# Scan stage: turned states as three rounded products, split by ScalarE and GpSimd, with the input sum on GpSimd

## The chip, the cores and the metric

The kernel runs on one core of one Trainium2 chip. The metric is device time in microseconds (us) of the whole program. Engines are named TensorE (PE in the profile, with its weight loads as PEld), VectorE (DVE), ScalarE (ACT), GpSimd (POOL) and SyncE (SP, which issues the DMAs).

## The reference, cut to what matters

`x` has shape (16, 1024, 256), float32. The reference adds four branches in turn, each to `x` and each of a layer norm of `x`: a state space layer, a feed-forward coupling, causal attention, and the feed-forward coupling again. The change touches the first one alone:

```python
# h = layernorm(x); Lbar = mag * exp(i * Lam_imag * dt), one complex decay for each of 64 states
nr = Lbar_r * sr - Lbar_i * si + bur          # bur, bui = h @ (dt * B_real).T, h @ (dt * B_imag).T
ni = Lbar_r * si + Lbar_i * sr + bui
y = SR @ C_real.T - SI @ C_imag.T + D * h
out = y @ W_out.T + b_out                     # x = x + out
```

The kernel turns the rotating complex recurrence into a real one. It multiplies the inputs by cos and sin of the angle of each step, adds the two products, runs a scan with a real decay, and multiplies the scanned states by cos and sin again. The outputs are matrix products with weights into which `C` and `W_out` are folded.

## The kernel before

The stage is `ssm_phase`. It has 32 chunks, two for each of the 16 sequences, of 512 steps of 256 features. A chunk is held as four tiles of 128 steps. Buffers are doubled: chunk n uses set k = n mod 2. In the steady state each engine works through one slot n of the main block in a fixed, written-out order; there is no planner, and the engines meet through semaphores alone.

- TensorE (`slot`, L493): `turn(n+1)` (L160) transposes the normalised rows (8 records at L166). `project(n+1)` (L462) makes the two input products `ssm_bu`, 8 matmuls of 512 columns with the rounded transposed input (L469) and 4 with its remainder (L474). `out(n)` (L478) makes four output tiles at L488: each has 4 products of `xnT` and 2 of `xnT_lo` with the rounded skip weights, and 2 full float32 products, `w_cos` with `out_cos_w` and `w_sin` with `out_sin_w`. A float32 product is two records in the trace.
- VectorE (`slot`, L435): `low(n+1)` (L145) takes the remainder of the transposed input, `normalise(n+2)` (L123) makes statistics and moments, `scan(n+1)` (L405) makes `u_cos`, `u_sin`, their sum `u` (L411), the scan (L413), `w_cos` (L419) and `w_sin` (L420). Then `scale(n+2)` (L136) normalises the rows in four `tensor_scalar` instructions (L141), and `residual(n)` (L422) adds the output to `xb` (L427).
- ScalarE: `evacuate(n)` (L151) copies and rounds the transposed input (L158), two instructions for each chunk.
- GpSimd: `chunk(n)` (L385) makes `var_eps` and `rstd` in `rstds` (L115, L117 and L121), then `xb` = `x` + bias in `residual_bias` (L393), which waits for `y` of chunk n-2.
- SyncE loads and stores the chunks (L361, L365).

"Rounded" is the type float32r, a float32 that TensorE takes in one pass. The skip weights are already held as a rounded part and the rounded remainder (`skip_parts`). In the block ahead of the main one VectorE makes these parts at L312 and L315, and the output weights at L316 and L317.

Of the kernel before, what the change touches and what calls it, by code (L numbers as in the profile page):

```python
# [57 lines left out]
def ssm_phase(nc, sem, identf, x, x1, log_lam, lam_imag, b_real, b_imag, c_real, c_imag, d_skip, log_dt,  # L58
# [15 lines left out]
    with ExitStack() as ctx:  # L74
        def sb(name, shape, dt=F32):
            return ctx.enter_context(nc.sbuf_tensor("ssm_" + name, shape, dt))
# [26 lines left out]
        w = [sb(f"w{k}", [P, CH]) for k in range(2)]  # L103
        w_cos = [sb(f"w_cos{k}", [P, CH]) for k in range(2)]
        w_sin = [sb(f"w_sin{k}", [P, CH]) for k in range(2)]
        turned_ps = ctx.enter_context(nc.psum_tensor("ssm_turned", [P, KT, CH], F32))
# [3 lines left out]
        (stats_done, moments_done, eps_added, rstd_ready, xn_ready, turned, xnT_ready, xnT_lo_ready, bu_ready, u_parts, u_ready,  # L110
         w_ready, w_turned, out_ready, xb_ready, y_ready, const_ready) = [sem("ssm_" + n) for n in (
             "stats_done", "moments_done", "eps_added", "rstd_ready", "xn_ready", "turned", "xnT_ready", "xnT_lo_ready", "bu_ready",
             "u_parts", "u_ready", "w_ready", "w_turned", "out_ready", "xb_ready", "y_ready", "const_ready")]

        def rstds(pool, n, k, old):  # L115
            pool.wait_ge(moments_done, n + 1)
# [53 lines left out]
        with ExitStack() as pre:  # L170
# [40 lines left out]
            with nc.Block() as block:  # L211
# [31 lines left out]
                def _(dve):  # L243
# [71 lines left out]
                        v.tensor_tensor(parts[1][:, :, :], w[:, :, :], parts[0][:, :, :], ALU.subtract)  # L315
                    v.tensor_copy(out_cos_w[:, :], m_ps[:, 0, 0:D])  # L316
                    step(v.tensor_copy(out_sin_w[:, :], m_ps[:, 1, 0:D]))  # L317

                @block.scalar
                def _(act):  # L320
# [31 lines left out]
        with nc.Block() as block:  # L352
# [29 lines left out]

            @block.gpsimd
            def _(pool):
                def chunk(n, it, k, old):  # L385
                    rstds(pool, n, k, old)
                    residual_bias(n, it, k, old)

                def residual_bias(n, it, k, old):
                    pool.wait_ge(x_loaded[k], 16 * it + 16)  # L390
                    if old:
                        pool.wait_ge(y_ready, n - 1)
                    nc.gpsimd.tensor_tensor(xb[k][:, :, :], xt[k][:, :, :],  # L393
                                            bias_row[:, :].unsqueeze(1).to_broadcast([P, TT, D]),
                                            ALU.add).then_inc(xb_ready, 1)

                residual_bias(0, 0, 0, False)
                chunk(1, 0, 1, False)
                with pool.Fori(1, n_steps) as it:
                    for k in range(2):  # L400
                        chunk(2 * it + k, it, k, True)

            @block.vector
            def _(dve):
                def scan(n, k, old):  # L405
                    cos_k, sin_k = cos_t[:, k * CH:(k + 1) * CH], sin_t[:, k * CH:(k + 1) * CH]
                    dve.wait_ge(bu_ready, n + 1)
                    nc.vector.tensor_tensor(u_cos[:, :], bu_ps[k][:, 0, :], cos_k, ALU.mult)
                    nc.vector.tensor_tensor(u_sin[:, :], bu_ps[k][:, 1, :], sin_k, ALU.mult).then_inc(u_parts, 1)
                    dve.wait_ge(u_parts, n + 1)  # L410
                    nc.vector.tensor_tensor(u[:, :], u_cos[:, :], u_sin[:, :], ALU.add).then_inc(u_ready, 1)  # L411
# [7 lines left out]
                    nc.vector.tensor_tensor(w_cos[k][:, :], w[k][:, :], cos_k, ALU.mult)  # L419
                    nc.vector.tensor_tensor(w_sin[k][:, :], w[k][:, :], sin_k, ALU.mult).then_inc(w_turned, 1)  # L420
# [10 lines left out]
                scale(dve, 1, 1, False)  # L431
                scan(0, 0, False)


                def slot(n, it, k, old, more):  # L435
                    low(dve, n + 1, 1 - k)
                    if more:
                        normalise(dve, n + 2, it + 1, k, True)
                    scan(n + 1, 1 - k, old or k == 1)
                    if more:  # L440
                        scale(dve, n + 2, k, True)
                    residual(n, it, k, old)

                slot(0, 0, 0, False, True)
                slot(1, 0, 1, False, True)
                with dve.Fori(1, n_steps - 1) as it:
                    for k in range(2):
                        slot(2 * it + k, it, k, True, True)
                it = n_steps - 1
                slot(2 * it, it, 0, True, False)  # L450
                residual(2 * it + 1, it, 1, True)

            @block.scalar
            def _(act):
                evacuate(act, 1, 1, False)
                with act.Fori(1, n_steps) as it:
                    for k in range(2):
                        evacuate(act, 2 * it + k, k, True)

            @block.tensor  # L460
            def _(pe):
# [1758 lines left out]
```

## Time and profile before

| what | value |
|---|---|
| median of 3 runs | 3762.95 us (3755.66 to 3763.63) |
| the profiled execution's own time | 3763.16 us |
| its span | 3761.3 us |
| busy, share of the span | PE 95%, PEld 62%, DVE 79%, ACT 58%, POOL 44% |
| the first stage | up to about 380 us of the span |

A row of a timeline gives the start, the duration, the engine, the line, the operation, what it writes and reads, how many were merged, and in brackets the idle time of the engine before it with what released it. Busy times of TensorE overlap, since matmuls are pipelined, so distances between starts are the better measure there. A row of busy time by stretches gives the stretch, its length, then the busy time and the instructions of PE, PEld, DVE, ACT and POOL, the granted clock of TensorE as a share, the DMA share and GB/s.

### The profile page before, as it was taken

To read this page: it belongs to the slowest core of one execution; us is meant where nothing else is said; L and a number is where in the kernel's file an instruction comes from. 1 tells how busy PE (TensorE), PEld (TensorE's weight loads), DVE (VectorE), ACT (ScalarE), POOL (GpSimd) and SP (SyncE) were. 2 spreads that over 40 slices of the span, in tenths; PEclk is the share of its full clock that TensorE was granted. 3 is DMA by queue.
4 is the path that set the end of the run, shared out by engine and by line. 5 is a ranking of instruction groups with operands and counts; after the bars stand their busy time and mean duration, and the time that the engine had idled before them with its cause. 6 is when DMAs were issued, how large, how long until landed. Compare 5 with 4: busy or idle time off the path is not lost. (4 is left out here: it accounts for less than half of the span.)

```text
span 3761.3 us, 76026 instructions
## 1 busy us (share of the span) xinstructions
PE 3560.0 (95%) x25550; PEld 2347.9 (62%) x25550; DVE 2952.9 (79%) x9275; ACT 2183.7 (58%) x4151; POOL 1666.4 (44%) x2027
## 2 busy tenths in 40 slices
PE   6999899999689999999999999999999998999997
PEld 5888666666455665566656656655666555666664
DVE  8998666766688888888888888888888893676775
ACT  1110456655337766766676667667667665656654
POOL 2332123223345556656555565565565511223323
PEclk9999899999879999999999999999999999999999
DMA  2333112111497978787887879788887832121211
GB/s 74 100 98 109 57 46 68 54 59 35 116 140 111 126 115 129 120 127 123 122 127 119 132 116 126 116 119 123 124 134 121 120 41 80 40 68 46 68 46 45
DMA packets 694291, 361.16 MB, mean 96 GB/s; under 512 B 297905, under 2 KB 660913, under 8 KB 693937
## 3 DMA queue, kind: packets, MB, share of 16 engines
q1 hardware_dynamic: 693936, 356.62, 53.5%
q8 instruction: 200, 3.28, 0.4%
q14 instruction: 155, 1.26, 0.2%
HBM read 204.49 MB, written 150.99 MB: 95 GB/s over the span
## 5 line engine op out<-in xcount | busy, mean ns | idle before, releaser
L1862 ACT ACTIVATE att_probs<-att_s 128x512 f32<-128x512 f32 x2304 | 1212.5, 601 | 461.2 <-PE att_s L2001 234.4
L1737 DVE CUSTOM_DVE_ANT_0 att_s<-att_s,att_above 128x384 f32<-128x384 f32 (+3 forms) x2048 | 950.2, 519 | 132.8 <-PE att_s L1981 127.1
L1981 PE MATMUL att_s<-att_ks,att_qs 48*128 48x512 f32 (+3 forms) x3072 | 896.0, 401 | 5.7 <-DVE att_maxima L1740 3.6
L2001 PE MATMUL att_s<-att_qs,att_ks 49*128 49x512 f32 (+3 forms) x3072 | 852.4, 373 | 20.5 <-DVE att_maxima L1737 5.2
L2001 PEld LDWEIGHTS att_s<-att_qs,att_ks 49*128 49x128 f32 x3072 | 487.6, 186 | 464.0 <-ACT att_probs L1862 271.6
L1740 DVE TENSOR_REDUCE att_maxima<-att_s 128x1 f32<-128x512 f32 x1024 | 661.9, 684 | 98.3 <-PE att_s L1981 93.2
L2029 PE MATMUL att_o_ps<-att_probs,att_vs 128*32 128x512 f32 (+3 forms) x6144 | 620.5, 497 | 25.1 <-ACT att_probs L1862 22.1
L1981 PEld LDWEIGHTS att_s<-att_ks,att_qs 48*128 48x128 f32 x3072 | 485.9, 189 | 26.4 <-DVE att_maxima L1737 8.9
L1097 PE MATMUL ffn_h2p<-ffn_h,ffn_w 128*128 128x512 f32 x768 | 365.0, 598 | 3.0 <-ACT ffn_h L968 0.9
L1951 PE MATMUL att_s<-att_mask,att_places 64*128 64x128 bf16 (+1 forms) x2560 | 327.7, 212 | 0.0
L1737 DVE DVE_READ_ACCUMULATOR2_ANT att_maxima<- 128x1 f32 x2048 | 293.0, 143 | 0.0
L946 ACT ACTIVATE ffn_uv<-ffn_uvp 128x512 f32<-128x512 f32 x256 | 153.1, 598 | 237.5 <-PE ffn_uvp L1072 237.5
L2029 PEld LDWEIGHTS att_o_ps<-att_probs,att_vs 128*32 128x32 f32 x6144 | 145.9, 108 | 222.9 <-issue 159.6
L1564 POOL CAST att_qs<-att_staged 113x1024 fp32r<-113x1024 f32 x128 | 253.7, 2005 | 0.0
L976 ACT ACTIVATE ffn_h<-ffn_turned,ffn_b 128x512 f32<-128x512 f32 x384 | 241.9, 684 | 13.5 <-PE ffn_turned L1088 11.6
L1564 POOL CAST att_ks<-att_staged 113x1024 fp32r<-113x1024 f32 x126 | 249.7, 2000 | 0.0
L968 ACT ACTIVATE ffn_h<-ffn_h2p,ffn_b 128x512 f32<-128x512 f32 x192 | 132.0, 687 | 197.8 <-PE ffn_h2p L1097 197.8
L1088 PEld LDWEIGHTS ffn_turned<-identf,ffn_uv 128*128 128x128 f32 x1536 | 174.8, 142 | 75.5 <-issue 53.9
L158 ACT ACTIVATE ssm_xnT<-ssm_turned 128x512 fp32r<-128x512 f32 x64 | 34.9, 595 | 313.7 <-PE ssm_turned L166 313.7
L1088 PE MATMUL ffn_turned<-identf,ffn_uv 128*128 128x128 f32 x1536 | 201.8, 274 | 10.2 <-DVE ffn_uv L823 8.0
L823 DVE SCALAR_TENSOR_TENSOR ffn_uv<-ffn_uv,ffn_c_pos 128x256 f32<-128x256 f32 x512 | 209.3, 483 | 2.3
L691 POOL TENSOR_TENSOR ffn_var_eps<-ffn_moments,ffn_eps 128x4 f32<-128x4 f32 x64 | 13.3, 208 | 433.4 <-DVE ffn_moments L776 433.4
(292 smaller groups left out, 6384.8 us busy)
## 6 DMA issues: line engine op xcount, KB each, us to landing
att_staged<-qk_scratch SPq DMA_DIRECT2D x768, 128.0 KB, 7.6
qk_scratch<-att_parts SPq DMA_DIRECT2D x128, 512.0 KB, 3.4
ffn_x<-x SPq DMA_DIRECT2D x64, 512.0 KB, 5.2
ssm_x<-in_L_attn_a_x_dram SPq DMA_DIRECT2D x32, 512.0 KB, 3.7
x<-ssm_y SPq DMA_DIRECT2D x32, 512.0 KB, 3.0
x<-ffn_y SPq DMA_DIRECT2D x32, 512.0 KB, 2.9
att_x<-x SPq DMA_DIRECT2D x32, 512.0 KB, 7.4
v_scratch<-att_v_tok SPq DMA_DIRECT2D x32, 512.0 KB, 5.3
```

What stands on the lines that cost most here:

```text
L823: last = v.scalar_tensor_tensor(out=new[:, t, 0:D], in0=old[:, t, D:2 * D], scalar=c_pos[i][j][:, t, k:k + 1], in1=old[:, t, 0:D], op0=ALU ...
L976: last = a(h1[k][:, f, :], turned_ps[:, f, :], ACT.Gelu, bias=b1[:, f:f + 1])
L1088: last = pe.transpose(turned_ps[:, f, t * P:(t + 1) * P], of[:, t, f * P:(f + 1) * P], identf[:, :])
L1097: last = mm(h2_ps[:, :], w2[:, f, :], h1[k][:, f, :], start=(f == 0), stop=(f == KT - 1))
L1564: last = g.tensor_copy(stack[0:ROWS, :].rearrange("p (t c) -> p t c", c=HD)[:, e * n:(e + 1) * n, :], staged[side][0:ROWS, :, e * n:(e + 1 ...
L1737: last = v.tensor_tensor_reduce(scores, scores, above[:, CH - w:CH], 1.0, -3.0e38, ALU.add, ALU.max, to)
L1740: last = v.tensor_reduce(to, scores, AX.X, ALU.max)
L1862: a(probs[u % PROBS][2 * g + p][:, 0:n], bank[:, 0:n], ACT.Exp).then_inc(exp_done, 1)
L1951: last = mm(blocks[:, at, GROUP * half:GROUP * (half + 1)], places[rows, 2 * (1 - k) + half, :], mask[rows, 1 - k, 0:len(cols), :], start= ...
L1981: last = mm(bank[:, col:col + w], rows_of(qs[buf], g, KROWS, p, BT * blk, BT * (blk + 1)), rows_of(ks[buf], g, KROWS, p, t0, t1), start=k ...
L2001: last = mm(bank[:, col:col + w], rows_of(ks[buf], g, SHIFT + 1, p, BT * j, BT * (j + 1)), rows_of(qs[buf], g, SHIFT + 1, p, t0, t1), star ...
L2029: last = mm(o_ps[32 * i:32 * i + 32, HD * (t0 - first_t):HD * (t1 - first_t)], vs[s][:, NBLK * head + j, :], probs[of % PROBS][i][:, col:c ...
```

## The change

The two float32 products of each output tile become six rounded ones. The weights `out_cos_w` and `out_sin_w` are split into two rounded parts ahead of the main block (four more VectorE instructions on 128x256). For the states, ScalarE rounds `w_cos` and `w_sin` (`round_turned`, after `evacuate` of the chunk behind), and GpSimd subtracts to get the remainders (`split`). TensorE's `out` waits for the second remainder. The sum `u` goes from VectorE to GpSimd (`add_parts`), and VectorE's `scale(n+2)` moves ahead of the scan, between `u_sin` and the wait for `u`.

```diff
+                def add_parts(n):
+                    pool.wait_ge(u_parts, n + 1)
+                    nc.gpsimd.tensor_tensor(u[:, :], u_cos[:, :], u_sin[:, :], ALU.add).then_inc(u_ready, 1)
+
+                def split(n, k):
+                    for m, turned_w in enumerate((w_cos[k], w_sin[k])):
+                        pool.wait_ge(w_hi_ready, 2 * n + m + 1)
+                        nc.gpsimd.tensor_tensor(w_lo[k][:, m, :], turned_w[:, :], w_hi[k][:, m, :].bitcast(F32),
+                                                ALU.subtract).then_inc(w_lo_ready, 1)
+
                 def chunk(n, it, k, old):
                     rstds(pool, n, k, old)
+                    add_parts(n - 1)
+                    split(n - 1, 1 - k)
                     residual_bias(n, it, k, old)
...
@@ VectorE, slot
-                    scan(n + 1, 1 - k, old or k == 1)
+                    turn_back(n + 1, 1 - k)
                     if more:
                         scale(dve, n + 2, k, True)
+                    scan(n + 1, 1 - k, old or k == 1)
                     residual(n, it, k, old)
...
@@ ScalarE
+                def round_turned(n, k):
+                    for m, turned_w in enumerate((w_cos[k], w_sin[k])):
+                        act.wait_ge(w_back, 2 * n + m + 1)
+                        nc.scalar.activation(w_hi[k][:, m, :], turned_w[:, :], ACT.Copy).then_inc(w_hi_ready, 1)
...
                         evacuate(act, 2 * it + k, k, True)
+                        round_turned(2 * it + k - 1, 1 - k)
...
@@ TensorE, out
-                    pe.wait_ge(w_turned, n + 1)
+                    pe.wait_ge(w_lo_ready, 2 * n + 2)
...
-                        terms += [(w_cos[k][:, cols], out_cos_w[:, :]), (w_sin[k][:, cols], out_sin_w[:, :])]
+                        terms += [(w_hi[k][:, m, cols], out_parts[i][:, m, :]) for m in range(2) for i in range(2)]
+                        terms += [(w_lo[k][:, m, cols], out_parts[0][:, m, :]) for m in range(2)]
```

`turn_back(n, k)` holds the two multiplications `u_cos` and `u_sin` that stood at the head of `scan`. For chunk 0 they stand after `scale(1)`. After the loop GpSimd does `add_parts` and `split` of the last chunk, and ScalarE its `round_turned`.

## Rows read from the trace of the kernel before

**Rows 1.** Busy time by stretches, in the steady stage.
```profile
60.00:160.00 100.00, 97.43 (x576) 84.98 (x575) 94.12 (x208) 9.78 (x18) 32.73 (x28) 1.00 0.31 99
```

**Rows 2.** Waits of VectorE and TensorE, 60 to 350 us: total, times, longest.
```profile
DVE ssm_y L427 <- PE ssm_out L488: 11.6, 28, 0.4
PE ssm_bu L469 <- ACT ssm_xnT L158: 7.8, 27, 0.3
```

**Rows 3.** Timeline of one slot, TensorE and ScalarE.
```profile
201.66 1.09 PE L166 MATMUL ssm_turned<-identf,ssm_xn 128*128 128x128 f32 x8
202.43 1.09 ACT L158 ACTIVATE ssm_xnT<-ssm_turned 128x512 fp32r<-128x512 f32 x2 [9.52 <-PE ssm_turned L166]
203.08 0.73 PE L469 MATMUL ssm_bu<-ssm_xnT,ssm_bu_p 128*128 128x512 f32 x2 [0.33 <-ACT ssm_xnT L158]
...
205.96 0.64 PE L488 MATMUL ssm_out<-ssm_skip_p,ssm_xnT 128*128 128x256 f32 x4
...
206.67 0.59 PE L488 MATMUL ssm_out<-ssm_out_cos_w,ssm_w_cos 128*128 128x256 f32 x2
...
207.34 0.82 PE L488 MATMUL ssm_out<-ssm_skip_p,ssm_xnT 128*128 128x256 f32 x4
...
212.25 1.04 PE L166 MATMUL ssm_turned<-identf,ssm_xn 128*128 128x128 f32 x8
```

**Rows 4.** Timeline of the same slot, VectorE.
```profile
201.96 1.23 DVE L427 TENSOR_TENSOR ssm_y<-ssm_out,ssm_xb 128x1024 f32<-128x1024 f32 x1 [0.43 <-PE ssm_out L488]
203.10 1.28 DVE L148 TENSOR_TENSOR ssm_xnT_lo<-ssm_turned,ssm_xnT 128x512 fp32r<-128x512 f32 x2
...
206.16 0.69 DVE L408 TENSOR_TENSOR ssm_u_cos<-ssm_bu,ssm_cos 128x512 f32<-128x512 f32 x1
...
207.48 0.69 DVE L411 TENSOR_TENSOR ssm_u<-ssm_u_cos,ssm_u_sin 128x512 f32<-128x512 f32 x1
208.21 1.22 DVE L413 TENSOR_TENSOR_SCAN ssm_w<-ssm_decay,ssm_u 128x512 f32<-128x512 f32 x1
209.46 0.69 DVE L419 TENSOR_TENSOR ssm_w_cos<-ssm_w,ssm_cos 128x512 f32<-128x512 f32 x1
...
210.67 1.38 DVE L141 TENSOR_SCALAR ssm_xn<-ssm_x,ssm_moments,ssm_rstd 128x256 f32<-128x256 f32 x4
212.45 1.22 DVE L427 TENSOR_TENSOR ssm_y<-ssm_out,ssm_xb 128x1024 f32<-128x1024 f32 x1 [0.40 <-PE ssm_out L488]
```

**Rows 5.** Timeline of the same slot, GpSimd.
```profile
203.33 2.42 POOL L393 TENSOR_TENSOR ssm_xb<-ssm_x,ssm_bias_row 128x1024 f32<-128x1024 f32 x1 [6.34 <-DVE ssm_y L427]
206.19 0.20 POOL L117 TENSOR_TENSOR ssm_var_eps<-ssm_moments,ssm_eps 128x4 f32<-128x4 f32 x1 [0.45 <-DVE ssm_moments L133]
206.47 1.01 POOL L121 TENSOR_TENSOR ssm_rstd<-ssm_var_eps,ssm_minus_half 128x4 f32<-128x4 f32 x1
```

**Rows 6.** Groups by line and form, GpSimd, whole span: busy, mean ns, idle before.
```profile
L1552 POOL TENSOR_TENSOR att_parts<-att_full,att_parts 128x512 fp32r<-128x512 f32 x116 | 148.6, 1281 | 9.3
```

**Rows 7.** Timeline at the head of the main block, GpSimd and VectorE.
```profile
37.39 2.35 POOL L393 TENSOR_TENSOR ssm_xb<-ssm_x,ssm_bias_row 128x1024 f32<-128x1024 f32 x1
37.46 3.41 DVE L141 TENSOR_SCALAR ssm_xn<-ssm_x,ssm_moments,ssm_rstd 128x256 f32<-128x256 f32 x4 [1.82 <-POOL ssm_rstd L121]
```

**Rows 8.** Timeline in the feed-forward stage, VectorE and GpSimd.
```profile
926.11 2.34 DVE L844 SCALAR_TENSOR_TENSOR ffn_y<-ffn_z,ffn_b_pos,ffn_y 128x128 f32<-128x128 f32 x1 [4.03 <-POOL ffn_y L729]
926.15 2.15 POOL L729 TENSOR_SCALAR ffn_y<-ffn_z,ffn_a_std,ffn_moments 128x256 f32<-128x256 f32 x4
```

**Rows 9.** Timeline of VectorE in the block ahead of the main one.
```profile
30.39 0.28 DVE L312 CAST ssm_bu_p<-ssm_bu_w 128x256 fp32r<-128x256 f32 x1
...
31.25 0.42 DVE L315 TENSOR_TENSOR ssm_bu_p<-ssm_bu_w,ssm_bu_p 128x256 fp32r<-128x256 f32 x1
```

**Rows 10.** Tile ssm_y: count, ns min/median/max, first and last start.
```profile
L427 DVE TENSOR_TENSOR ssm_y<-ssm_out,ssm_xb x32: 1224/1225/1226, 54.2 to 378.1; 128x1024 f32<-128x1024 f32 x32
```

**Rows 11.** Timeline of VectorE late in the stage.
```profile
359.79 1.23 DVE L427 TENSOR_TENSOR ssm_y<-ssm_out,ssm_xb 128x1024 f32<-128x1024 f32 x1 [0.40 <-PE ssm_out L488]
```

More of the change, by code:

```diff
@@ L105, in ssm_phase @@
         w_sin = [sb(f"w_sin{k}", [P, CH]) for k in range(2)]
+        w_hi, w_lo = [[sb(f"{n}{k}", [P, 2, CH], F32R) for k in range(2)] for n in ("w_hi", "w_lo")]
+        out_parts = [sb(f"out_p{i}", [P, 2, D], F32R) for i in range(2)]
         turned_ps = ctx.enter_context(nc.psum_tensor("ssm_turned", [P, KT, CH], F32))
@@ L110, in ssm_phase @@
         (stats_done, moments_done, eps_added, rstd_ready, xn_ready, turned, xnT_ready, xnT_lo_ready, bu_ready, u_parts, u_ready,
-         w_ready, w_turned, out_ready, xb_ready, y_ready, const_ready) = [sem("ssm_" + n) for n in (
+         w_ready, w_back, w_hi_ready, w_lo_ready, out_ready, xb_ready, y_ready, const_ready) = [sem("ssm_" + n) for n in (
              "stats_done", "moments_done", "eps_added", "rstd_ready", "xn_ready", "turned", "xnT_ready", "xnT_lo_ready", "bu_ready",
-             "u_parts", "u_ready", "w_ready", "w_turned", "out_ready", "xb_ready", "y_ready", "const_ready")]
+             "u_parts", "u_ready", "w_ready", "w_back", "w_hi_ready", "w_lo_ready", "out_ready", "xb_ready", "y_ready", "const_ready")]
         def rstds(pool, n, k, old):
@@ L317, in _ @@
                     step(v.tensor_copy(out_sin_w[:, :], m_ps[:, 1, 0:D]))
+                    turns = (out_cos_w, out_sin_w)
+                    for m, turn_w in enumerate(turns):
+                        last = v.tensor_copy(out_parts[0][:, m, :], turn_w[:, :])
+                    step(last)
+                    for m, turn_w in enumerate(turns):
+                        last = v.tensor_tensor(out_parts[1][:, m, :], turn_w[:, :], out_parts[0][:, m, :], ALU.subtract)
+                    step(last)
                 @block.scalar
@@ L401, in _, with turn_back @@
                         chunk(2 * it + k, it, k, True)
+                add_parts(n_chunks - 1)
+                split(n_chunks - 1, 1)
             @block.vector
             def _(dve):
+                def turn_back(n, k):
+                    cos_k, sin_k = cos_t[:, k * CH:(k + 1) * CH], sin_t[:, k * CH:(k + 1) * CH]
+                    dve.wait_ge(bu_ready, n + 1)
+                    dve.wait_ge(u_ready, n)
+                    nc.vector.tensor_tensor(u_cos[:, :], bu_ps[k][:, 0, :], cos_k, ALU.mult)
+                    nc.vector.tensor_tensor(u_sin[:, :], bu_ps[k][:, 1, :], sin_k, ALU.mult).then_inc(u_parts, 1)
                 def scan(n, k, old):
                     cos_k, sin_k = cos_t[:, k * CH:(k + 1) * CH], sin_t[:, k * CH:(k + 1) * CH]
[L407 to L411, printed above, removed]
                     dve.wait_ge(u_ready, n + 1)
@@ L418, in scan @@
                         dve.wait_ge(out_ready, n - 1)
-                    nc.vector.tensor_tensor(w_cos[k][:, :], w[k][:, :], cos_k, ALU.mult)
-                    nc.vector.tensor_tensor(w_sin[k][:, :], w[k][:, :], sin_k, ALU.mult).then_inc(w_turned, 1)
+                    nc.vector.tensor_tensor(w_cos[k][:, :], w[k][:, :], cos_k, ALU.mult).then_inc(w_back, 1)
+                    nc.vector.tensor_tensor(w_sin[k][:, :], w[k][:, :], sin_k, ALU.mult).then_inc(w_back, 1)
                 def residual(n, it, k, old):
@@ L431, in _ @@
                 scale(dve, 1, 1, False)
+                dve.wait_ge(bu_ready, 1)
+                cos_0, sin_0 = cos_t[:, 0:CH], sin_t[:, 0:CH]
+                nc.vector.tensor_tensor(u_cos[:, :], bu_ps[0][:, 0, :], cos_0, ALU.mult)
+                nc.vector.tensor_tensor(u_sin[:, :], bu_ps[0][:, 1, :], sin_0, ALU.mult).then_inc(u_parts, 1)
                 scan(0, 0, False)
@@ L454, in _ @@
             def _(act):
+                def round_turned(n, k):
+                    for m, turned_w in enumerate((w_cos[k], w_sin[k])):
+                        act.wait_ge(w_back, 2 * n + m + 1)
+                        nc.scalar.activation(w_hi[k][:, m, :], turned_w[:, :], ACT.Copy).then_inc(w_hi_ready, 1)
                 evacuate(act, 1, 1, False)
+                round_turned(0, 0)
                 with act.Fori(1, n_steps) as it:
@@ L458, in _ @@
                         evacuate(act, 2 * it + k, k, True)
+                        round_turned(2 * it + k - 1, 1 - k)
+                round_turned(n_chunks - 1, 1)
             @block.tensor
```

## The prediction

> **What bounds the stage now.** I read the busy time by stretches first, then the waits, then the timeline of one slot of each engine. Up to 380 us only this stage runs, and nothing else in the program changes, so only its length counts. Between 60 and 160 us TensorE is busy 97.4% at a granted clock of 1.00 (2.4 GHz) and VectorE 94.1%, while ScalarE has 10% and GpSimd 33% [rows 1]. Only two waits recur: VectorE's residual waits about 0.4 us for TensorE's output, 28 times, and TensorE about 0.3 us for ScalarE's copy, 27 times [rows 2]. So TensorE sets the pace and VectorE is close behind. The residual starts at 54.2 for chunk 0 [rows 10] and at 359.79 for chunk 29 [rows 11], 29 slots of 10.54 us.
>
> The slot shows how tight it is. TensorE goes from one transposition to the next in 212.25 - 201.66 = 10.59 us [rows 3]. VectorE's `scale` ends at 210.67 + 1.38 = 212.05, 0.2 us before the transposition that needs it [rows 3, 4]. GpSimd is idle most of the slot, with 2.42 + 0.20 + 1.01 us of work [rows 5].
>
> **What TensorE gains.** In the first output tile the six rounded products take 206.67 - 205.96 = 0.71 us, 0.118 each. The record at 207.34, the head of the second tile, is put some 0.2 early against the matmuls before it, so I take the whole: from 205.96 to 212.25 the four tiles take 6.29 us, 1.57 each [rows 3]. Twelve rounded products take 12 x 0.118 = 1.42, four tiles 5.67. That is 0.62 us less for each slot, if nothing else came in.
>
> **What VectorE gains.** The sum `u` and the wait for it go: 208.21 - 207.48 = 0.73 us [rows 4], and some 0.1 us of the wait before it. Without its wait of 0.43 a slot is about 10.1 us of work, so about 9.2 is left.
>
> **What GpSimd takes on.** Three instructions on 128x512 with two inputs in SBUF: one sum and two differences. The same form with the same types takes 1281 ns in the attention stage, 116 times [rows 6]. I take 1.28 us, and 1.25 from start to start, since on this engine the next one starts some 0.03 us before the end. GpSimd's work grows from 3.6 to 7.4 us a slot, well within 10.5. But its order now makes a loop, and I price that loop.
>
> **The blockade inside the loop.** `add_parts` follows `rstd` on GpSimd and reads two tiles in SBUF, and VectorE's `scale` is released by the same `rstd`. The head of the main block has this very meeting: GpSimd's `xb` starts at 37.39, the four `scale` instructions start at 37.46 and take 3.41 us [rows 7] instead of 1.38 [rows 4]. They lose 2.03 us to an instruction of 2.35, that is its duration less 0.32. In the feed-forward stage a VectorE instruction with two SBUF inputs takes 2.34 us while four GpSimd instructions run for 2.15 [rows 8]. So `scale` doesn't run beside the sum, it waits for it: 1.28 - 0.32 = 0.96 us. From below the price is nothing (the two overlap), from above it is the whole 1.28; I take 0.96, because rows 7 have the same two kinds of instruction in the same order.
>
> The Trainium skill, SBUF — State Buffer, section "Who interferes with whom", has the rule: VectorE in a two-port mode and GpSimd share one pair of ports, the one that issues first holds it for its whole instruction, and the other fully blocks. By that rule the sum with the blockade is 3784.5 us, and by the opposite (both run side by side) it would be 3772.5. Rows 7 agree with the rule. It speaks against putting the sum under `scale`.
>
> **The loop.** Let 0 be the start of the sum on GpSimd.
> - `scale` starts at 0.07 [rows 7], takes 1.30 up to the next start (1.38 less an overlap of 0.08 as between instructions elsewhere) and 0.96 more. The scan starts at 2.33.
> - `w_cos` starts 1.25 later and ends after 0.69 [rows 4]: 4.27. In every second chunk the scan is 0.06 longer; on the mean 4.30.
> - ScalarE starts 0.08 later (a handoff, estimated from 206.19 against the end of the moments) and hands on after 0.65, as 202.43 to 203.08 [rows 3]; GpSimd starts about 0.05 later still than TensorE did: 5.08.
> - The two differences, 1.25 each: 7.58. Then `xb`, which follows in GpSimd's order, 2.35 from start to start (2.40 less the overlap) [rows 5, 7]: 9.93.
> - `var_eps` to `rstd` 0.28, `rstd` 1.01 less 0.03 [rows 5]: 11.19. Then the next sum starts, since VectorE's `u_parts` are long there.
>
> In some slots `rstd` starts 0.08 later after `var_eps`, so I take 11.22 us a slot, 0.68 more than 10.54. `var_eps` doesn't wait for the moments in it: VectorE is at the residual at 2.33 + 1.25 + 0.61 + 0.60 = 4.79, at `low` 1.14 later, and has the moments 3.06 after that [rows 4], at 8.99, when `xb` holds GpSimd until 9.93. VectorE then stands still before `scale` for about 1 us a slot. TensorE starts its transposition at about 2.5, has projected by 7.7 (its last remainder products wait for `low`), and ends the output at 7.7 + 5.67 = 13.4, that is 2.2 in the next slot; it isn't on the path. The 0.62 us it saved go into idle time. Its idle pieces stay about 1 us, and I expect no drop of the clock; the bound above is a half clock for part of each slot, several us a slot, which no row of the steady stage supports.
>
> **The new wait of `out`.** It needs the second difference, at 5.08 + 2.53 = 7.61 plus a handoff. That ties with the end of the projection, so it costs nothing while the loop above rules. Queued behind it on TensorE are the next transpositions.
>
> **Head and tail.** Four more VectorE instructions on 128x256 ahead of the main block: starts 0.20 apart for casts and 0.34 for differences, with two semaphore steps, 1.3 us, with nothing to hide them [rows 9], where a start-to-start distance is 0.08 less than the duration. In the main block `scale(1)` no longer meets `xb` (it comes back 2.0 us), but the sum of chunk 0 comes after `scale(1)`, and the second `rstd` after both differences and `xb(1)`. From 37.42 + 1.3 I add 0.04 + 1.30 + 1.28 + 0.08 + 1.28 + 0.05 + 1.25 + 0.69 + 0.08 + 0.70 + 2.50 + 2.35 + 0.28 + 1.01 and come to 51.6, and the first residual at 51.6 + 4.8 = 56.4, against 54.2 [rows 10]: +2.2 us. At the end the last two chunks take 378.1 - 359.8 = 18.3 us now [rows 10, 11]; there the last sum follows `xb(31)` at 9.9, the second difference ends at about 16.5, the output takes 5.7, and the last residual starts 17.7 after that of chunk 29: -0.6 us.
>
> **The sum.** 29 x 0.68 = 19.7, + 2.2 - 0.6 = +21.3 us. On the profiled execution's 3763.16 us that gives 3784.5. That execution stands 0.2 us from the median of the runs shown, so the same number is compared with them.
>
> **Rivals.**
> - No blockade: `scale` runs beside the sum. The loop through GpSimd is then 11.22 - 0.96 + 0.1 = 10.4, and another one decides: `round_turned` stands behind `evacuate` on ScalarE. From a transposition's start to the end of the second copy is 203.52 - 201.66 = 1.86, the rounding with handoffs 0.70, the differences 2.53, the handoff 0.06, the output 5.67: 10.82 us [rows 3, 6]. That is 29 x 0.28 + 1.2 = +9.3, 3772.5 us. Against it stand rows 7.
> - VectorE wins the port: the sum then waits for all of `scale`, and the scan starts at 0.07 + 1.38 + 1.28 = 2.7 instead of 2.33. The slot is 11.6, the time 3796. For it: the two are released by the same instruction and 0.07 us decides. Against it: rows 7 show GpSimd first. The same page says that issue order decides who blocks, and that gives this case no other number.
> - The gain arrives: TensorE stays the pacer and its 0.62 us a slot come through, 29 x -0.62 + 1.6 = -16.4, 3747 us. This needs both differences before the projection ends, 4.3 us after the transposition's start, so each at 0.8 us or less instead of 1.28, and the loop through `xb` below 10. For it: GpSimd is idle two thirds of the slot now. Against it: 116 instructions of that form at 1281 ns.
> - The products don't become cheaper than they were: without a rounded rate for them TensorE would need 12 x 0.118 plus more, but the loop on GpSimd hides up to 0.3 us a slot of it; about 3785 to 3790.
>
> **Chances.** The forecast has 0.60, no blockade 0.14, VectorE first 0.12, the gain 0.08, the rest (TensorE dearer, clock) 0.06. The forecast's own spread is 3777 to 3791 (a slot of 11.0 to 11.45). The range reaches down to the case without blockade and up to that with VectorE first: 3769 to 3797. What can be told from no change here is about 0.2%, 7.5 us. Faster by more gets 0.08, within it 0.09 (the low side of the case without blockade), slower 0.83.
>
> **What would show it.** The distance between residuals in the steady stage: 11.2 us, against 10.8, 11.6 or 9.9 in the other cases. `scale` at L141's place would take about 2.3 us for four, starting 0.07 us after the sum; VectorE would wait about 1 us a slot for `rstd`; GpSimd's only long idle time, about 3.8 us, would stand before the first difference, ended by ScalarE; the output would take 5.7 us and TensorE be busy below 92%. A residual that still waits for the output, or `scale` at 1.38 beside the sum, would prove me wrong.

## The result and the profile after

The changed kernel takes 3789.17 us (median of 4 runs, 3782.70 to 3790.77), the kernel before 3760.01 us (median of 4, 3755.66 to 3763.63). The ratio is 1.0069, 95% interval 1.0056 to 1.0083. That is slower, clear of the noise but by less than 1%: about 26 us by the ratio, 29.2 between the medians. The forecast was 3784.5. The profiled execution took 3790.77 us with a span of 3788.9, 27.6 more than the span before.

The line of the residual's tile gives the length of the stage:

```profile
L452 DVE TENSOR_TENSOR ssm_y<-ssm_out,ssm_xb x32: 1214/1217/1225, 56.9 to 401.1; 128x1024 f32<-128x1024 f32 x32
```

Against 54.2 to 378.1 [rows 10] the first residual comes 2.7 us later, and the stretch from the first to the last grows from 323.9 to 344.2 us, by 20.3. Together 23.0 of the 27.6 us lie in the stage. The other 4.6 lie behind it, where both kernels execute the same instructions; they are taken up below, under "The rest of the span".

Busy time of the same stretch as [rows 1], then the waits of 60 to 360 us (total, times, longest):

```profile
60.00:160.00 100.00, 90.98 (x610) 77.64 (x610) 88.89 (x187) 20.67 (x36) 65.23 (x54) 1.00 0.30 92
```
```profile
POOL ssm_w_lo L401 <- ACT ssm_w_hi L488: 101.3, 27, 3.8
...
DVE ssm_xn L143 <- POOL ssm_rstd L123: 30.7, 27, 1.3
PE ssm_bu L512 <- DVE ssm_xnT_lo L150: 16.8, 26, 0.7
...
PE ssm_bu L507 <- ACT ssm_xnT L160: 7.8, 27, 0.3
```

TensorE fell from 97.4% to 91.0% and VectorE from 94.1% to 88.9%: neither is the bound any more. GpSimd is at 65%, so by busy time it isn't either. The waits show what is: VectorE stands still before the row scaling in every slot until GpSimd's `rstd` is there, and GpSimd stands still before its first difference until ScalarE has rounded. Each waits for the other in turn, which is a loop. VectorE's residual no longer waits for TensorE, as it did 28 times in [rows 2].

The timeline of one slot, VectorE, answers to [rows 4]:

```profile
202.68 1.22 DVE L452 TENSOR_TENSOR ssm_y<-ssm_out,ssm_xb 128x1024 f32<-128x1024 f32 x1
...
209.17 2.34 DVE L143 TENSOR_SCALAR ssm_xn<-ssm_x,ssm_moments,ssm_rstd 128x256 f32<-128x256 f32 x4 [1.18 <-POOL ssm_rstd L123]
211.43 1.27 DVE L438 TENSOR_TENSOR_SCAN ssm_w<-ssm_decay,ssm_w,ssm_u 128x512 f32<-128x512 f32 x1
212.74 0.69 DVE L444 TENSOR_TENSOR ssm_w_cos<-ssm_w,ssm_cos 128x512 f32<-128x512 f32 x1
...
213.95 1.21 DVE L452 TENSOR_TENSOR ssm_y<-ssm_out,ssm_xb 128x1024 f32<-128x1024 f32 x1
```

and GpSimd's, to [rows 5]:

```profile
209.10 1.28 POOL L396 TENSOR_TENSOR ssm_u<-ssm_u_cos,ssm_u_sin 128x512 f32<-128x512 f32 x1
214.17 1.29 POOL L401 TENSOR_TENSOR ssm_w_lo<-ssm_w_cos,ssm_w_hi 128x512 fp32r<-128x512 f32 x1 [3.78 <-ACT ssm_w_hi L488]
...
216.65 2.40 POOL L414 TENSOR_TENSOR ssm_xb<-ssm_x,ssm_bias_row 128x1024 f32<-128x1024 f32 x1
219.01 0.20 POOL L119 TENSOR_TENSOR ssm_var_eps<-ssm_moments,ssm_eps 128x4 f32<-128x4 f32 x1
219.29 1.01 POOL L123 TENSOR_TENSOR ssm_rstd<-ssm_var_eps,ssm_minus_half 128x4 f32<-128x4 f32 x1
220.27 1.29 POOL L396 TENSOR_TENSOR ssm_u<-ssm_u_cos,ssm_u_sin 128x512 f32<-128x512 f32 x1
```

Follow the loop once around. The sum starts at 209.10 and `scale` at 209.17, but `scale` takes 2.34 instead of 1.38, so the scan waits for it until 211.43. `w_cos` ends at 213.43, ScalarE rounds it, the two differences start at 214.17 and 215.41, `xb` follows, and the next `rstd` lets the next sum start at 220.27, 11.17 after the first. No instruction in this circle has slack, and between `scale` and the rounding there is a second way of the same length. TensorE's transposition waits for `scale` too (it starts 0.13 us after `scale` ends), and ScalarE's copies of it, which stand ahead of the rounding, end when `w_cos` is there (213.50 and 213.43). By these rows a faster scan alone would gain nothing; that wasn't tested.


```profile
212.41 1.09 ACT L160 ACTIVATE ssm_xnT<-ssm_turned 128x512 fp32r<-128x512 f32 x2 [8.97 <-PE ssm_turned L168]
213.46 0.63 ACT L488 ACTIVATE ssm_w_hi<-ssm_w_cos 128x512 fp32r<-128x512 f32 x1
```

TensorE, against [rows 3]: its output now takes from 205.72 to about 211.4.

```profile
205.72 0.64 PE L527 MATMUL ssm_out<-ssm_skip_p,ssm_xnT 128*128 128x256 f32 x4
...
207.15 0.63 PE L527 MATMUL ssm_out<-ssm_skip_p,ssm_xnT 128*128 128x256 f32 x4
...
211.64 1.09 PE L168 MATMUL ssm_turned<-identf,ssm_xn 128*128 128x128 f32 x8
```

### The profile page after: what moved, and what is told of

It is laid out like the page before. It is cut to its first block and busy times, and to the rows that moved or that the text cites. A ratio compares the mean times of both kernels' runs of the same rounds, so it can differ in the third digit from the quotient of the medians.

```text
span 3788.9 us, 76791 instructions
## 1 busy us (share of the span) xinstructions
PE 3564.4 (94%) x25806; PEld 2341.1 (62%) x25806; DVE 2952.6 (78%) x9247; ACT 2221.8 (59%) x4215; POOL 1784.0 (47%) x2123
## 3 DMA queue, kind: packets, MB, share of 16 engines
q14 instruction: 156, 1.28, 0.1%
## 5 line engine op out<-in xcount | busy, mean ns | idle before, releaser
L1127 PE MATMUL ffn_turned<-identf,ffn_uv 128*128 128x128 f32 x1536 | 202.5, 275 | 10.2 <-DVE ffn_uv L862 7.9
```

What stands on the lines that cost most here:

```text
L1127: last = pe.transpose(turned_ps[:, f, t * P:(t + 1) * P], of[:, t, f * P:(f + 1) * P], identf[:, :])
```

## The experiments

"First to last" below is from the start of the first residual to that of the last, 31 slots. "Steady slot" is the mean distance between the residuals of chunks 4 and 29, 25 slots; single slots differ from it, by up to 0.15 us in most kernels and by 0.55 in e9. (The prediction's 10.54 for the kernel before and 11.22 for the change count from chunk 0; counted so, the change measures 11.21.) Ratios are to the kernel before, run on the same chip, with the 95% interval. The experiments ran on four chips, on which the median of the kernel before is between 3755.8 and 3763.7 us, so rows are compared by ratio or by slot. The three single runs (e2, e6, e7) have no interval; the kernel before took 3755.8 there.

| kernel | us | ratio | first to last | steady slot |
|---|---|---|---|---|
| before | 3760.01 | 1 | 323.9 | 10.52 |
| after | 3789.17 | 1.0069 (1.0056 to 1.0083) | 344.2 | 11.20 |
| e1_sum_vector | 3771.54 | 1.0022 (1.0008 to 1.0037) | 331.5 | 10.76 |
| e2_half_sum | 3773.36 | one run | 332.7 | 10.76 |
| e3_products_alone | 3765.14 | 1.0004 (0.9990 to 1.0018) | 323.7 | 10.51 |
| e4_scale_first | 3764.95 | 0.9999 (0.9985 to 1.0012) | 322.0 | 10.48 |
| e5_both_alone | 3740.79 | 0.9939 (0.9920 to 0.9958) | 302.4 | 9.85 |
| e6_bias_late | 3814.97 | one run | 381.5 | 12.41 |
| e7_vector_first | 3793.13 | one run | 344.3 | 11.21 |
| e8_round_first | 3745.74 | 0.9974 (0.9957 to 0.9991) | 314.3 | 10.23 |
| e9_rows_on_scalar | 3768.84 | 1.0023 (1.0009 to 1.0037) | 327.1 | 10.70 |
| e10_mean_first | 3742.32 | 0.9944 (0.9926 to 0.9963) | 304.4 | 9.84 |
| e11_rows_halved | 3746.55 | 0.9954 (0.9940 to 0.9968) | 306.3 | 9.91 |

### e1: the sum back on VectorE

```diff
 GpSimd, chunk
-                    add_parts(n - 1)
...
 VectorE, turn_back
+                    dve.wait_ge(u_parts, n + 1)
+                    nc.vector.tensor_tensor(u[:, :], u_cos[:, :], u_sin[:, :], ALU.add).then_inc(u_ready, 1)
```

> The changed kernel with the sum u back on VectorE, between u_sin and scale; everything else as changed. Theory (the loop through GpSimd with the sum and the blockade in it sets the slot): scale falls back from 2.34 to 1.38 us for four, GpSimd's loop loses 1.25 for the sum and 0.96 for the blockade and is near 9.7, and the next loop decides, the one in which ScalarE rounds only behind its evacuation: 10.7 to 10.85 us from residual to residual, some 3770 to 3775 us. Rival (the blockade is a side effect, and the differences in front of the output's wait set the slot by themselves): the slot stays at 11.1 to 11.2 and the time near 3785.

Measured: `scale` back at 1.38, a slot of 10.76, 12.7 us less from first to last than the changed kernel. The sum on GpSimd costs 0.44 us a slot although its own blockade is 0.96, because a second loop stands right behind. VectorE's and ScalarE's timelines show it:

```profile
203.31 1.38 DVE L143 TENSOR_SCALAR ssm_xn<-ssm_x,ssm_moments,ssm_rstd 128x256 f32<-128x256 f32 x4 [0.91 <-POOL ssm_rstd L123]
```
```profile
205.90 1.09 ACT L160 ACTIVATE ssm_xnT<-ssm_turned 128x512 fp32r<-128x512 f32 x2 [8.65 <-PE ssm_turned L168]
206.87 0.63 ACT L486 ACTIVATE ssm_w_hi<-ssm_w_cos 128x512 fp32r<-128x512 f32 x1
```

The rounding stands behind the two copies, these behind the transposition, that behind the output of the chunk before, and that output behind the differences of the rounding. This is the loop of 10.82 us that the prediction priced under "no blockade". The expectation for e1 put GpSimd's own loop near 9.7, with the sum's 1.25 taken off as well as the blockade. That was wrong: `scale` waits for `rstd` and not for the sum, so the sum's own length isn't in the loop, only the blockade is (see e8).

### e2: the sum over half the columns

The other half of `u` stays zero, so half of the sum is left out.

```diff
-   nc.gpsimd.tensor_tensor(u[:, :], u_cos[:, :], u_sin[:, :], ALU.add)
+   nc.gpsimd.tensor_tensor(u[:, 0:CH // 2], u_cos[:, 0:CH // 2], u_sin[:, 0:CH // 2], ALU.add)
```

> The changed kernel with GpSimd's sum over half of the columns; the other half of u stays zero, so half of the sum is left out. Dose test of the blockade: the sum takes 0.65 us, and the four scale instructions should take 1.38 + 0.65 - 0.32 = 1.7 us instead of 2.34. The loop through GpSimd is 11.2 - 0.64 = 10.6, so ScalarE's order decides at 10.8: some 3770 to 3775 us. If the blockade were a fixed price (a stall on meeting), scale would stay at 2.3 and the slot above 11.

VectorE's and GpSimd's timelines:

```profile
205.07 1.79 DVE L143 TENSOR_SCALAR ssm_xn<-ssm_x,ssm_moments,ssm_rstd 128x256 f32<-128x256 f32 x4 [1.34 <-POOL ssm_rstd L123]
```
```profile
205.00 0.74 POOL L397 TENSOR_TENSOR ssm_u<-ssm_u_cos,ssm_u_sin 128x256 f32<-128x256 f32 x1
```

`scale` loses 0.41 us to a sum of 0.74 (0.33 less), as it lost 0.96 to one of 1.28 (0.32 less). So the loss follows the length of GpSimd's instruction. The slot shrinks only to 10.76, that of e1, because ScalarE's loop takes over: the rounding again starts when the copies end, 0.1 to 0.2 us after `w_cos` is there.

### e3, e4 and e5: what the gains are worth without GpSimd and ScalarE

e3 gives the kernel before the six rounded products. e4 gives it `scale` ahead of the scan. e5 has both. e3 and e5 leave the split of the states out: VectorE writes `w_cos` and `w_sin` rounded, and the two products with the remainder take the rounded tile again. They do TensorE's work of the change without that of ScalarE and GpSimd, so they measure time and don't compute the reference's values.

```diff
 e3 and e5
+        w_cos = [sb(f"w_cos{k}", [P, CH], F32R) for k in range(2)]
+        w_sin = [sb(f"w_sin{k}", [P, CH], F32R) for k in range(2)]
...
-                        terms += [(w_cos[k][:, cols], out_cos_w[:, :]), (w_sin[k][:, cols], out_sin_w[:, :])]
+                        terms += [(turned_w[m][:, cols], out_parts[i][:, m, :]) for m in range(2) for i in range(2)]
+                        terms += [(turned_w[m][:, cols], out_parts[0][:, m, :]) for m in range(2)]
...
 e4 and e5
-                    scan(n + 1, 1 - k, old or k == 1)
+                    turn_back(n + 1, 1 - k)
                     if more:
                         scale(dve, n + 2, k, True)
+                    scan(n + 1, 1 - k, old or k == 1)
```

> The kernel before with six rounded products for each output tile in place of the two float32 ones, and nothing on ScalarE or GpSimd: w_cos and w_sin are written rounded by VectorE, and the remainder products take the rounded tile again, so the split is left out. Order of VectorE and the sum as before. Theory of the prediction (TensorE sets the pace of the kernel before): its 0.62 us a slot come through in whole or in half, 9.9 to 10.25 us from residual to residual, 3742 to 3753 us. Rival (a loop of VectorE sets it: scale, transposition, ScalarE's copy, low, with the residual's wait for the output only falling into the same gap): the slot stays at 10.5, and with 1.3 us more ahead of the main block the time is that of before, 3760 to 3763.

> The kernel before with scale moved ahead of the scan and nothing else. If VectorE's loop through scale and low set the pace, it is now broken, but TensorE's own slot of 10.49 us (0.33 of a wait in it) stands right behind it: 10.48 to 10.50 a slot, 1 to 2 us off the time. If TensorE set the pace from the start, nothing changes: 10.53. Either way within 0.1% of before; the run counts for the wait of low, which should go from tied with ScalarE's copy to none.

> The kernel before with the rounded products (without the split, as in the run of the products alone) and scale ahead of the scan. If VectorE's loop sets the pace of the kernel before, only the two together bring the gain: 9.95 to 10.1 us a slot, 3744 to 3748 us, while the products alone bring nothing. If TensorE alone sets it, this run equals that of the products alone within 0.1%.

e3 is the surprise: TensorE's 0.62 us a slot went, and the time did not move. VectorE's and TensorE's timelines:

```profile
202.80 1.38 DVE L142 TENSOR_SCALAR ssm_xn<-ssm_x,ssm_moments,ssm_rstd 128x256 f32<-128x256 f32 x4
204.09 1.22 DVE L435 TENSOR_TENSOR ssm_y<-ssm_out,ssm_xb 128x1024 f32<-128x1024 f32 x1
205.71 1.29 DVE L149 TENSOR_TENSOR ssm_xnT_lo<-ssm_turned,ssm_xnT 128x512 fp32r<-128x512 f32 x2 [0.40 <-ACT ssm_xnT L159]
```
```profile
204.32 1.09 PE L167 MATMUL ssm_turned<-identf,ssm_xn 128*128 128x128 f32 x8 [0.46 <-DVE ssm_xn L142]
```

The residual no longer waits, but the 0.40 us of idle time has only moved one instruction on, to `low`. TensorE now waits for `scale` before it transposes. There is a second loop, as long as TensorE's own work: `scale`, the transposition, ScalarE's copy, `low`, and then VectorE's work up to the next `scale`. It was in [rows 3, 4] already: `scale` ended 0.2 us before the transposition, and `low` started right after the copy.

e4 breaks that loop alone (the scan and the two multiplications move behind `scale`, beside the transposition), and then TensorE is what is left: the residual waits for its output 29 times, 15.5 us in all.

```profile
DVE ssm_y L430 <- PE ssm_out L493: 15.5, 29, 0.6
```

The slot is 10.48, and the time again stays. e5 breaks both and saves 22 us, with a slot of 9.85 in which VectorE works without a recurring wait, a little better than expected (9.95 to 10.1). So the gain of the change is there, but each half is worth next to nothing without the other. Per slot: 10.52 before, 9.85 with both gains, 10.76 with the splits on ScalarE and GpSimd (e1), 11.20 with the sum there too.

### e6 and e7: who holds the port, and for how long

e6 puts `xb` right behind the sum, ahead of the differences. e7 lets the sum start only when the first of the four `scale` instructions is done.

```diff
 e6
                     add_parts(n - 1)
+                    if late:
+                        residual_bias(n - 1, it if k else it - 1, 1 - k, k == 1 or long)
                     split(n - 1, 1 - k)
-                    residual_bias(n, it, k, old)
...
 e7
+                if t == 0:
+                    last.then_inc(scale_begun, 1)
...
+                        pool.wait_ge(scale_begun, n + 2)
                     nc.gpsimd.tensor_tensor(u[:, :], u_cos[:, :], u_sin[:, :], ALU.add).then_inc(u_ready, 1)
```

> The changed kernel with GpSimd's xb of the chunk before put between the sum and the differences, where GpSimd stands idle for 3.7 us of each slot. Nothing is left out. By GpSimd's idle time alone xb's 2.35 us leave its loop: 8.9 us, and ScalarE's order decides at 10.8, 3772 us. By the port: the sum and xb run back to back for 3.6 us, scale is held for all of it but 0.32 (3.3 us), or the scan, w_cos and w_sin with their two SBUF inputs are; the slot then gets longer, 12 to 12.8 us, 3810 to 3835 us, and the four scale instructions take 4.5 to 4.7 us.

> The changed kernel, but GpSimd's sum waits until the first of the four scale instructions is done, so that VectorE has the port first. This is the third rival of the prediction. If the port is held by back-to-back instructions, the sum waits for all four: scale takes 1.38 again, the sum takes up to 2.2 us, the scan starts about 2.8 after rstd instead of 2.33, and the slot is 11.6 to 11.7, some 3800 us. If the sum gets in between two scale instructions, one of the three left is held: scale stays at 2.3 us and the slot is 11.5 to 11.6. If the port isn't what holds them, both run side by side: 10.8, 3772 us.

e6, VectorE's timeline (the first row merges all four), then the four alone of the next slot (ns min/median/max), then GpSimd's timeline:

```profile
199.05 4.41 DVE L143 TENSOR_SCALAR ssm_xn<-ssm_x,ssm_moments,ssm_rstd 128x256 f32<-128x256 f32 x4 [0.32 <-POOL ssm_rstd L123]
```
```profile
L143 DVE TENSOR_SCALAR ssm_xn<-ssm_x,ssm_moments,ssm_rstd x4: 403/889/2476, 211.4 to 215.5; 128x256 f32<-128x256 f32 x4
```
```profile
198.99 1.29 POOL L396 TENSOR_TENSOR ssm_u<-ssm_u_cos,ssm_u_sin 128x512 f32<-128x512 f32 x1
200.23 2.43 POOL L415 TENSOR_TENSOR ssm_xb<-ssm_x,ssm_bias_row 128x1024 f32<-128x1024 f32 x1
```

Both GpSimd instructions hold `scale` up: one of the four takes about 1.38 us, another 2.48, two are normal. The loss is 4.41 - 1.38 = 3.03 us. The instruction that the sum held completes when the sum is over, and only the next is held by `xb`: GpSimd doesn't keep the port across the two. The slot grows to 12.41, as expected by the port: VectorE is busy or held 97% of the time, and GpSimd now waits up to 1.6 us a slot for VectorE's moments.

e7, VectorE's and GpSimd's timelines:

```profile
208.62 2.36 DVE L143 TENSOR_SCALAR ssm_xn<-ssm_x,ssm_moments,ssm_rstd 128x256 f32<-128x256 f32 x4 [1.17 <-POOL ssm_rstd L123]
```
```profile
209.18 1.32 POOL L400 TENSOR_TENSOR ssm_u<-ssm_u_cos,ssm_u_sin 128x512 f32<-128x512 f32 x1 [0.59 <-DVE ssm_xn L143]
```

VectorE starts first by 0.56 us here, and yet the sum gets in between two instructions of `scale` and takes 1.32, and the third of the four takes 1.38. The slot, 11.21, is that of the changed kernel. The expectation had this case at 11.5 to 11.6. The sum starts 0.6 us later behind `rstd` than in the changed kernel, but that only shortens GpSimd's idle time before the first difference, to 3.1 us from 3.8. Who is first makes no difference, so the rival "VectorE wins the port, 11.6 us" has no price here.

### e8: ScalarE rounds before it copies

```diff
 ScalarE, on e1
-                        evacuate(act, 2 * it + k, k, True)
                         round_turned(2 * it + k - 1, 1 - k)
+                        evacuate(act, 2 * it + k, k, True)
```

> As the run with the sum back on VectorE, and ScalarE rounds the turned states of the chunk in hand before it evacuates the next transposition, not behind it. Theory (the 10.80 us a slot of that run is the loop transposition, evacuation, rounding, two differences, output): the loop is cut, the differences are ready before the projection ends, and the slot falls to 10.2 to 10.4 us, 3752 to 3760 us. Rival (the loop through rstd, scale, scan, the differences and xb on GpSimd, some 10.3 by its rows but priced too low, is what takes 10.8): nothing changes, 3771.

Moving the rounding ahead of the copies, on an engine that is 20% busy, is worth 17.2 us from first to last against e1. The slot of 10.23 is within the expected 10.2 to 10.4. (The expected 3752 to 3760 us were missed by 6 us; the kernel before takes 3755.8 on this chip, 7 us less than on that of e1.) It is also the changed kernel's 11.20 less the blockade of 0.96, so what is left is GpSimd's loop without the sum. VectorE's timeline, then GpSimd's:

```profile
206.00 1.38 DVE L143 TENSOR_SCALAR ssm_xn<-ssm_x,ssm_moments,ssm_rstd 128x256 f32<-128x256 f32 x4
...
208.55 0.69 DVE L440 TENSOR_TENSOR ssm_w_cos<-ssm_w,ssm_cos 128x512 f32<-128x512 f32 x1
```
```profile
199.81 1.28 POOL L397 TENSOR_TENSOR ssm_w_lo<-ssm_w_cos,ssm_w_hi 128x512 fp32r<-128x512 f32 x1 [4.08 <-ACT ssm_w_hi L486]
...
204.95 1.01 POOL L123 TENSOR_TENSOR ssm_rstd<-ssm_var_eps,ssm_minus_half 128x4 f32<-128x4 f32 x1
209.98 1.28 POOL L397 TENSOR_TENSOR ssm_w_lo<-ssm_w_cos,ssm_w_hi 128x512 fp32r<-128x512 f32 x1 [4.02 <-ACT ssm_w_hi L486]
```

`rstd` ends at 205.96, `scale` starts 0.04 later, `w_cos` ends at 209.24, and the next difference starts at 209.98, 10.17 after the last. (The slots with the longer scan take 10.30.) The waits on VectorE are too short to be listed (about 0.1 us), and it is 97% busy between 60 and 160 us, so its own order is as long as this circle; which of the two a further change would have to shorten wasn't tested.

### e9, e10 and e11: row scaling on ScalarE

If `scale` isn't on VectorE, the scan doesn't stand behind `rstd`. e9 does it as an activation with scale `rstd` and bias `-mean * rstd`, for which GpSimd makes `minus_mean` and `shift`. e10 moves `minus_mean` ahead of `rstd`. e11 lets VectorE and ScalarE scale two tiles each.

```diff
 e9, on e8
+            nc.gpsimd.tensor_scalar(minus_mean[k][:, :], moments[k][:, :, 0], -1.0, 0.0, ALU.mult, ALU.add).then_inc(rstd_done, 1)
+            nc.gpsimd.tensor_tensor(shift[k][:, :], minus_mean[k][:, :], rstd[k][:, :], ALU.mult).then_inc(rstd_ready, 1)
...
+                last = nc.scalar.activation(xn[k][:, t, :], xt[k][:, t, :], ACT.Identity, bias=shift[k][:, t:t + 1],
+                                            scale=rstd[k][:, t:t + 1])
...
+                        scale_rows(act, 2 * it + k, it, k, True)
                         round_turned(2 * it + k - 1, 1 - k)
                         evacuate(act, 2 * it + k, k, True)
```

> A version meant to beat both. As the run with ScalarE rounding first and the sum on VectorE, and the row scaling goes from VectorE to ScalarE, as one activation for each of the four tiles with rstd as scale and minus mean times rstd as bias; GpSimd makes that bias with two more small instructions. No instruction of VectorE in a two-port form is left in the slot, and VectorE has 8.6 us of work. By the rows: transposition to ScalarE's copy 1.35, projection 2.9, output 5.67, so TensorE's own 9.9 us decide, if the differences (ready some 2.5 us after w_cos and w_sin) come before the projection ends. 9.85 to 10.0 us a slot, 3736 to 3744 us, 0.4 to 0.6% under before. Rival (ScalarE gets too full in its order: four activations of about 0.5 us, two roundings and two copies, 4.3 us, hold back the evacuation): 10.2 us or more, no better than the run before it.

e9 missed its expectation by 25 us. GpSimd's timeline, then VectorE's:

```profile
210.17 1.01 POOL L125 TENSOR_TENSOR ssm_rstd<-ssm_var_eps,ssm_minus_half 128x4 f32<-128x4 f32 x1
211.16 1.18 POOL L126 TENSOR_SCALAR ssm_minus_mean<-ssm_moments 128x4 f32<-128x4 f32 x1
212.43 0.71 POOL L128 TENSOR_TENSOR ssm_shift<-ssm_minus_mean,ssm_rstd 128x4 f32<-128x4 f32 x1
```
```profile
211.13 1.23 DVE L449 TENSOR_TENSOR_SCAN ssm_w<-ssm_decay,ssm_u 128x512 f32<-128x512 f32 x1
212.39 0.69 DVE L455 TENSOR_TENSOR ssm_w_cos<-ssm_w,ssm_cos 128x512 f32<-128x512 f32 x1
```

Two instructions on 128x4 take 1.18 and 0.71 us, where `var_eps` of that size takes 0.20. The first lies under the scan and ends with it, the second under `w_cos`; both of VectorE's have two inputs in SBUF. Here VectorE holds GpSimd up, 1.5 us a slot, and ScalarE waits for `shift`.

> As the run with the rows on ScalarE, but GpSimd's first small instruction for the bias (minus mean) goes ahead of rstd, where VectorE reads PSUM and one SBUF tile. In that run it started beside the scan and took 1.15 to 1.18 us instead of 0.2, and the second one 0.71: VectorE's instructions with two SBUF inputs held GpSimd. By that theory the first costs 0.2 here and the second 0.2 to 0.8, and GpSimd's loop (bias, ScalarE's four activations 2.08, rounding 0.65, differences 2.5, xb 2.35, rstd 1.5) falls from 10.8 to 9.4 to 10.0, so that TensorE's 9.9 decide: 9.9 to 10.1 us a slot, 3738 to 3746 us. Rival (the four activations hold back the rounding whatever GpSimd does): 10.5 or more.

> As the run with minus mean first, but VectorE scales two of the four tiles and ScalarE the other two. VectorE's work is 10.15 - 0.65 = 9.5 us a slot, ScalarE is done with its two before w_cos is there, so neither is in GpSimd's loop. TensorE's 9.9 us decide: 9.9 to 10.0, 3738 to 3745 us. If the second small GpSimd instruction is held by the sum and by VectorE's two scale instructions until the scan, ScalarE's half comes 1 us later and the slot is 10.1 to 10.2, as with rounding first alone.

e10, GpSimd's timeline and the waits of 60 to 360 us:

```profile
208.85 0.20 POOL L122 TENSOR_SCALAR ssm_minus_mean<-ssm_moments 128x4 f32<-128x4 f32 x1
209.06 1.01 POOL L126 TENSOR_TENSOR ssm_rstd<-ssm_var_eps,ssm_minus_half 128x4 f32<-128x4 f32 x1
210.15 0.54 POOL L128 TENSOR_TENSOR ssm_shift<-ssm_minus_mean,ssm_rstd 128x4 f32<-128x4 f32 x1
```
```profile
DVE ssm_y L463 <- PE ssm_out L539: 32.9, 30, 1.1
...
PE ssm_bu L519 <- ACT ssm_xnT L175: 7.3, 29, 0.3
```

`minus_mean` is back at 0.20, the slot falls to 9.84, and VectorE waits 1.1 us a slot for TensorE, which is 97.5% busy between 60 and 160 us. Now TensorE does set the pace, with the gain of the rounded products in it. This version leaves nothing out of what the changed kernel computes and is faster than both kernels: 0.9944 of the kernel before (0.9926 to 0.9963), where the changed kernel has 1.0069. That is 0.6%. e11 is no better (0.9954, 0.9940 to 0.9968).

## Why the prediction was right, and where it was wrong

- **The loop.** The timeline from the start of the sum, predicted and measured: scan 2.33 and 2.33, `w_cos` ends 4.30 and 4.33, first difference 5.08 and 5.07, `xb` 7.58 and 7.55, `var_eps` 9.93 and 9.91, next sum 11.19 and 11.17. The average slot was put at 11.22 and is 11.21 by the same count. e2 (sum halved) scales the loss, and e8 (sum away and ScalarE's order turned) has the loop less 0.96. e1 alone doesn't show it, since another loop sets its slot.
- **The blockade.** 0.96 predicted, 0.96 measured (2.34 against 1.38), and scaled in e2. The Trainium skill, SBUF — State Buffer, section "Who interferes with whom", says that the engine that issues first has the shared ports for its whole instruction. The trace agrees for one instruction, all but 0.32 us of it; e6 and e7 show that a row of such instructions does not keep them.
- **TensorE's and VectorE's gains.** The output takes 5.7 us as predicted (tiles at 205.72 and 207.15), and both gains went into idle time: TensorE at 91%, the wait for `rstd` about 1.1 us a slot where 1 was predicted. The granted clock stayed at 1.00 in the steady slots, and `out` doesn't wait for the second difference.
- **The sizes, and one step that failed.** The 29 slots from chunk 0 to chunk 29 grew by 19.4 us where 19.7 was put. The head grew by 2.7 where 2.2 was put. The last two chunks went the other way: -0.6 was put, and from the residual of chunk 29 (381.90) to the last (401.14) it is 19.24 us against 18.35 before, +0.9. There the step "I expect no drop of the clock" failed. TensorE stood still for 2.92 us before the output of the last chunk, until the second difference was there; from 395 to 400 us its granted clock is 0.67, between its two levels, and the four output tiles take 7.4 us instead of 5.7 (TensorE's timeline, then the busy time of the stretch). Without these 1.7 us the term would have been -0.8. So the total inside the stage, 23.0 where 21.3 was put, is off by this more than by anything else.

```profile
393.69 0.71 PE L527 MATMUL ssm_out<-ssm_skip_p,ssm_xnT 128*128 128x256 f32 x4 [2.92 <-POOL ssm_w_lo L401]
```
```profile
395.00:400.00 5.00, 5.00 (x31) 5.00 (x31) 0.00 (x0) 0.00 (x0) 0.00 (x0) 0.67 0.00 0
```

- **The rest of the span.** From the last residual to the end it is 3383.2 us before and 3387.8 after. The work there is unchanged, and 3.6 of the 4.6 us lie in the attention stage, which takes 2120.1 us before and 2123.7 after (first `att_qs` to last `att_x`). In the thirteen profiled executions, all with the same attention code, it takes 2112.0 (e6) to 2128.2 us (e7). So the 4.6 us are within what single executions differ by, and no run ties them to the change. What makes the executions differ stays open. The granted clock between 3000 and 3600 us doesn't explain it: it is 0.98 before and 0.95 after (the seventh figure, in the row of after below), but also 0.95 in e8, which has the shortest rest of all (3373.2).

```profile
3000.00:3600.00 600.00, 573.18 (x3378) 375.49 (x3376) 393.60 (x1242) 357.12 (x690) 148.15 (x308) 0.95 0.24 60
```

- **Wrong: "So TensorE sets the pace and VectorE is close behind."** The only recurring wait of VectorE was for TensorE, and I took that for proof. e3 and e4 show two loops tied within 0.05 us (10.51 with TensorE's shortened, 10.48 with VectorE's broken, 10.52 with both), so that taking 0.62 us off TensorE gave nothing. The forecast didn't fall with it, because it didn't use that step: it followed the new loop through all engines. But the rival "the gain arrives" was put on TensorE's time alone, and as the order stood, that gain also needed `scale` ahead of the scan (e4, e5).
- **Wrong: "VectorE wins the port", 11.6 us, with a chance of 0.12.** I let the sum wait for all four `scale` instructions. e7 makes exactly that meeting, and the sum doesn't wait for the four: it starts within the second and takes 1.32 us instead of 1.28.
- **Right as a mechanism: "no blockade", 10.82.** e1 has a slot of 10.76 by the ScalarE order that was named there. The same order is what makes the change lose even without the sum (1.0022), and turning it round makes a small gain of the loss (e8, 0.9974).
- **Luck.** The prediction followed `scale`, scan and `w_cos` to the rounding, and didn't look at the copies that stand ahead of the rounding on ScalarE. They end at the same moment (213.50 against 213.43). Had that way been longer, the slot would have been longer than forecast, by a path that the prediction had only in its rival.
- **How near it came.** The profiled execution took 6.3 us more than the 3784.5 forecast for it: 1.7 inside the stage, 4.6 behind it, where nothing was put.

## What to carry to other kernels

Before a helper engine with idle time takes on work, follow the order of its instructions as a circle through every engine and back to itself: an engine that is 20% or 65% busy can set the pace by where an instruction stands in its queue, and in e8 moving ScalarE's rounding ahead of its copies was worth 0.53 us a slot, nearly as much as the 0.62 us of arithmetic saved. A wait that recurs on the second busiest engine doesn't prove what binds; make that one operation cheaper by itself and see whether the wait vanishes or only moves to the next instruction. Where VectorE and GpSimd meet, place by pairs of instructions: for the pairs seen here a meeting costs nearly the whole of the other's instruction, even for a tile of 128x4. And don't take a clock read in the steady state for the ends of a stage.

## What the runs showed of the hardware

- A blocked VectorE instruction loses the GpSimd instruction's duration less about 0.32 us: 0.41 for 0.74, 0.96 for 1.28, 2.03 for 2.35 [rows 7]. With these forms the port is given anew for each instruction, on both sides (e6: 1.38 and 2.48 us in one row of four; e7: a sum of 1.32 between two of VectorE's). It isn't always so: in [rows 8] one VectorE instruction stood through four of GpSimd's in a row. What makes the difference wasn't tested.
- It works the other way too: beside VectorE's scan, product or sum with two inputs in SBUF, GpSimd instructions on 128x4 take 1.15 to 1.18, 0.71 and 0.50 to 0.54 us instead of 0.20 (e9, e10). In e1 `rstd` starts under VectorE's sum and takes 1.28 us in the median; in e8 it starts 0.3 us ahead of the sum and takes its usual 1.01. The same page of the Trainium skill has this for VectorE's instructions with two SBUF inputs in general; the numbers are these.
- After 2.92 us without work in the changed kernel, TensorE's granted clock was 0.67 between 395 and 400 us, and four output tiles took 7.4 us; at a clock of 1.00 they took 5.7.
